# Graph network kernel: sorted message rows in bins padded to 512 rows, returned 1024 rows at a time

## What is computed

```python
def _L2_gnn_ref(x, bases, comps, alpha, edge_index, edge_type):
    row, col = edge_index[0], edge_index[1]          # src, dst
    deg = jax.ops.segment_sum(ones, row, num_segments=n)
    deg_inv = where(deg > 0, rsqrt(maximum(deg, 1.0)), 0.0)
    norm = deg_inv[row] * deg_inv[col]
    h_j = x[col]
    c_e = comps[edge_type]
    hj_b = c_e[:, :, None] * h_j[:, None, :]
    msg = jnp.einsum('ebd,bdf->ef', hj_b, bases)
    msg = msg * alpha[edge_type] * norm[:, None]
    return jax.ops.segment_sum(msg, row, num_segments=n)
```

## Time and profile before

| | us |
|---|---|
| three runs | 8993.05, 9007.82, 9013.69 |
| median | 9007.82 |
| the profiled execution, its own time | 8996.33 |
| its span in the trace | 8994.6 |

### The profile page before, as it was taken

The page is one execution under the profiler, slowest core; times in us unless marked ns, Lnnn a source line. Parts: engine busy times, 40 slices in busy tenths (PEclk is TensorE's granted clock), DMA queues, the critical chain, the costliest instruction groups (busy, mean ns, idle before and its releaser), DMA issues. The chain is left out here.

```text
span 8994.6 us, 165062 instructions
## 1 busy us (share of the span) xinstructions
PE 6838.9 (76%) x39312; PEld 5322.2 (59%) x39312; DVE 5025.3 (56%) x13644; ACT 1795.2 (20%) x5149; POOL 5985.1 (67%) x6303
## 2 busy tenths in 40 slices
PE   2766667676777777776777788886773899999997
PEld 2666566565555454454555577775662677777776
DVE  6445545455666666664222256654445567677666
ACT  1111111111222121222222222220002122222221
POOL 3777777776777777775777777772001777777774
PEclk7555555555767777777777799996665555555555
DMA  6344444443333333332222255553444333333332
GB/s 195 122 142 132 137 142 127 142 133 96 88 85 90 85 89 89 85 90 81 82 84 83 83 152 162 164 155 99 109 107 128 91 92 92 90 92 90 93 91 63
DMA packets 886407, 979.31 MB, mean 109 GB/s; under 512 B 139646, under 2 KB 711216, under 8 KB 886063
## 3 DMA queue, kind: packets, MB, share of 16 engines
q1 hardware_dynamic: 592437, 482.50, 18.3%
q0 software_dynamic: 200960, 418.41, 17.4%
q10 hardware_dynamic: 92794, 76.22, 2.8%
HBM read 649.26 MB, written 333.71 MB: 109 GB/s over the span
## 5 line engine op out<-in xcount | busy, mean ns | idle before, releaser
L2160 POOL DMA_INDIRECT soft_rows<-proj,soft_slot x1564 | 1501.1, 960 | 1269.5 <-ACT soft_slot L2181 823.6
L755 POOL DMA_INDIRECT L_rows<-H,L_slot x1568 | 1487.5, 949 | 613.3 <-issue 601.4
L1575 POOL DMA_INDIRECT sorted<-msg_out,msg_idx x1564 | 1497.9, 958 | 494.3 <-issue 451.4
L1029 POOL DMA_INDIRECT L_rows<-H,L_slot x1568 | 1484.6, 947 | 479.6 <-issue 437.7
L893 PE MATMUL L_sum<-L_onehot,L_rows 128*128 128x64 f32 x3136 | 705.9, 400 | 590.6 <-DMA L_rows<-H,L_slot 564.0
L1664 PEld LDWEIGHTS msg_ps_msg<-msg_hb,msg_lhs 128*128 128x128 f32 x6272 | 944.2, 238 | 194.1 <-issue 193.5
L893 PEld LDWEIGHTS L_sum<-L_onehot,L_rows 128*128 128x128 f32 x3136 | 648.6, 306 | 653.2 <-issue 497.5
L1619 DVE SCALAR_TENSOR_TENSOR msg_lhs<-msg_dst_sp,msg_node,msg_ps_c 128x512 f32<-128x512 f32 x784 | 550.6, 744 | 864.2 <-ACT msg_dst_sp L1588 805.0
L1664 PE MATMUL msg_ps_msg<-msg_hb,msg_lhs 128*128 128x128 f32 x6272 | 1031.7, 332 | 0.3 <-DVE msg_lhs L1619 0.3
L1673 PE MATMUL msg_ps_sum<-msg_back,msg_lo_hot 128*128 128x128 f32 x3936 | 699.0, 339 | 180.2 <-DVE sums_r L1639 154.1
L2289 PE MATMUL soft_ps_sum<-soft_onehot,soft_x 128*128 128x64 f32 x3136 | 752.2, 422 | 85.1 <-DVE sums_b L2406 82.4
(11 more groups left out here) (394 smaller groups left out, 11283.3 us busy)
## 6 DMA issues: line engine op xcount, KB each, us to landing
sorted<-L_zeros SPq DMA_DIRECT2D x394, 330.0 KB
msg_back<-sorted SPq DMA_DIRECT2D x492, 264.0 KB
L_rows<-H,L_slot POOLq DMA_INDIRECT x3136
msg_hb<-HB SPq DMA_DIRECT2D x392, 128.0 KB
soft_at_in<-in_edge_attr_dram SPq DMA_DIRECT2D x195, 256.0 KB
HB<-L_prod ACTq DMA_DIRECT2D x49, 512.0 KB, 3.0
sorted<-msg_out,msg_idx POOLq DMA_INDIRECT x1564
soft_rows<-proj,soft_slot POOLq DMA_INDIRECT x1564
```

The costliest lines, as they stand in the source:

```text
L755: pool.indirect_dma_start(rows[:, k, j, :], None, t["H0"], bass.IndirectOffsetOnAxis(ap=slot[:, k, j:j + 1], axis=0)).then_inc(gathered[k] ...
L1029: pool.indirect_dma_start(rows[:, k, j, :], None, t["H1"], bass.IndirectOffsetOnAxis(ap=slot[:, k, j:j + 1], axis=0)).then_inc(gathered[k] ...
L1575: pool.indirect_dma_start(t["sorted"], bass.IndirectOffsetOnAxis(ap=idx[:, s, j:j + 1], axis=0), out[:, s, j, :], None, **({} if w is None ...
L2160: pool.indirect_dma_start(rows[:, s % SC, j, :], None, t["proj"], bass.IndirectOffsetOnAxis(ap=slot[:, s, j:j + 1], axis=0)).then_inc(gath ...
```

## The change

- `UNIT` is 512 rows, and a block is one unit. A block is therefore one accumulation of four matmuls, one lookup in `unit_col`, and one addition.
- Because bins are padded to 512 rows, the table grows from 252,416 rows (492 blocks) to 301,568 rows (588 blocks). Each zeroing piece of phase 0 grows from 330 to 396 KB per group, and the pieces outside the loop go from three to one.
- `CUT` goes from 25/49 to 22/49 of the groups (group 200 to 176). The sets are 46 for the first part and 52 (312 blocks) for the second. The turns with blocks beside the groups begin at turn 46 of 98 instead of 52.
- `back` holds three pairs of blocks. One transfer brings 1024 rows (528 KB), issued at every second block, once the pair three before it has been multiplied.
- The lookup is taken out of `gain` into a step of its own (`find_columns`), ahead of `find_own`.
- The accumulator is set to zero after the groups of the first part instead of at the start of the phase.
- A few `nop`s on SP.

```diff
-UNIT = 2 * P
-BLOCK = 2 * UNIT
+UNIT = 4 * P
...
-        self.CUT = self.NGP // GB * 25 // 49
+        self.CUT = self.NGP // GB * 22 // 49
...
-        self.SETS = [-(-units // (2 * BQ)) for units in most]
-        self.BASE = [0, self.SETS[0] * BQ * BLOCK]
-        self.FIRST_UNIT = [0, self.SETS[0] * BQ * 2]
-        self.ROWS = sum(self.SETS) * BQ * BLOCK
+        self.SETS = [-(-units // BQ) for units in most]
+        self.BASE = [0, self.SETS[0] * BQ * UNIT]
+        self.FIRST_UNIT = [0, self.SETS[0] * BQ]
+        self.ROWS = sum(self.SETS) * BQ * UNIT
...
-        HI, NU = S.NT, max(S.SETS) * BQ * 2
+        HI, NU = S.NT, max(S.SETS) * BQ
...
-            link(v.tensor_scalar(units_i[:, :], units_i[:, :], 8, None, ALU.arith_shift_right))
+            link(v.tensor_scalar(units_i[:, :], units_i[:, :], 9, None, ALU.arith_shift_right))
...
-        back, lo_hot = sb("back", [P, R3, 4, WR]), sb("lo_hot", [P, R3, 4, P])
+        back, lo_hot = sb("back", [P, R3, 8, WR]), sb("lo_hot", [P, R3, 4, P])
...
             def return_rows(i, q):
-                b = i * BQ + q
-                sp.wait_ge(totalled, b + 1)
-                sp.nop(nofuse=True)
-                sp.dma_start(back[:, q % R3, :, :], tiles_of(t["sorted"], b * 4, 4)).then_inc(returned[q % R3], 16)
+                if q % 2 == 0:
+                    b = i * BQ + q
+                    sp.wait_ge(totalled, b + 2)
+                    sp.nop(nofuse=True)
+                    sp.dma_start(back[:, q // 2, :, :], tiles_of(t["sorted"], b * 4, 8)).then_inc(returned[q // 2], 16)
...
-            link(v.memset(acc, 0.0), False)
...
+            def clear_sums(turns, k):
+                if k < 2:
+                    v.memset(acc, 0.0).then_inc(prep, 1)
+                    v.wait_ge(prep, link.n + 1)
...
             def find_own(i, q):
                 b = i * BQ + q
-                v.wait_ge(returned[q % R3], (i * (BQ // R3) + q // R3) * 16 + 16)
-                v.wait_ge(totalled, b + 1)
+                v.wait_ge(returned[q // 2], i * 16 + 16)
+                v.wait_ge(totalled, b + 1 + BQ - R3)
...
+            def find_columns(i, q):
+                b = i * BQ + q
+                cols[q] = v.value_load(t["unit_col"][0:1, ds(b, 1)], min_val=0, max_val=(S.NT + 2) * P)
+
             def gain(i, q):
                 b = i * BQ + q
-                for u in range(2):
-                    at = v.value_load(t["unit_col"][0:1, ds(b * 2 + u, 1)], min_val=0, max_val=(S.NT + 2) * P)
-                    v.wait_ge(totalled, b + 1 + R3)
-                    v.wait_ge(gained, b * 2 + u + 2 * R2)
-                    v.tensor_tensor(acc[:, ds(at, P)], acc[:, ds(at, P)], ps_sum[q % R2][:, u * P:(u + 1) * P], ALU.add).then_inc(gained, 1)
-            with_blocks(v, S, t, [(0, make_lhs)], [(0, find_own), (2, gain)])
+                at = cols.pop(q)
+                v.wait_ge(totalled, b + 1 + BQ)
+                v.wait_ge(gained, b + R2)
+                v.tensor_tensor(acc[:, ds(at, P)], acc[:, ds(at, P)], ps_sum[q % R2][:, 0:P], ALU.add).then_inc(gained, 1)
+            with_blocks(v, S, t, [(0, make_lhs)], [(2, find_columns), (0, find_own), (2, gain)], after=clear_sums)
...
                 pe.wait_ge(hot_made, b + 1)
-                pe.wait_ge(gained, 2 * b + 2)
+                pe.wait_ge(gained, b + 1)
                 for k in range(4):
-                    mm = pe.matmul(ps_sum[q % R2][:, k // 2 * P:(k // 2 + 1) * P], lo_hot[:, q % R3, k, :], back[:, q % R3, k, 0:F],
-                                   start=(k % 2 == 0), stop=(k % 2 == 1))
+                    mm = pe.matmul(ps_sum[q % R2][:, 0:P], lo_hot[:, q % R3, k, :], back[:, q // 2, q % 2 * 4 + k, 0:F],
+                                   start=(k == 0), stop=(k == 3))
```

More of the change, by code:

```diff
@@ L1608, in _ @@
             v.sem_inc(lhs_made, R2)
-            v.sem_inc(gained, 2 * R2)
+            v.sem_inc(gained, R2)
+            cols = {}
+            def clear_sums(turns, k):
+                if k < 2:
+                    v.memset(acc, 0.0).then_inc(prep, 1)
+                    v.wait_ge(prep, link.n + 1)
             def make_lhs(i, r, w, s):
@@ L1623, in find_own @@
                 b = i * BQ + q
-                v.wait_ge(returned[q % R3], (i * (BQ // R3) + q // R3) * 16 + 16)
-                v.wait_ge(totalled, b + 1)
-                own, columns = bcast(back[:, q % R3, :, F], 2, P), bcast(ps_columns[:, 0:P], 1, 4)
+                v.wait_ge(returned[q // 2], i * 16 + 16)
+                v.wait_ge(totalled, b + 1 + BQ - R3)
+                own, columns = bcast(back[:, q // 2, q % 2 * 4:q % 2 * 4 + 4, F], 2, P), bcast(ps_columns[:, 0:P], 1, 4)
                 if t["widely"][0]:
@@ L1631, in find_own @@
                 make.then_inc(hot_made, 1)
+            def find_columns(i, q):
+                b = i * BQ + q
+                cols[q] = v.value_load(t["unit_col"][0:1, ds(b, 1)], min_val=0, max_val=(S.NT + 2) * P)
             def gain(i, q):
                 b = i * BQ + q
-                for u in range(2):
-                    at = v.value_load(t["unit_col"][0:1, ds(b * 2 + u, 1)], min_val=0, max_val=(S.NT + 2) * P)
-                    v.wait_ge(totalled, b + 1 + R3)
-                    v.wait_ge(gained, b * 2 + u + 2 * R2)
-                    v.tensor_tensor(acc[:, ds(at, P)], acc[:, ds(at, P)], ps_sum[q % R2][:, u * P:(u + 1) * P], ALU.add).then_inc(gained, 1)
-            with_blocks(v, S, t, [(0, make_lhs)], [(0, find_own), (2, gain)])
-            v.wait_ge(gained, 2 * NB + 2 * R2)
+                at = cols.pop(q)
[3 more added lines that the diff above has]
+            with_blocks(v, S, t, [(0, make_lhs)], [(2, find_columns), (0, find_own), (2, gain)], after=clear_sums)
+            v.wait_ge(gained, NB + R2)
         @block.tensor
@@ L1646, in _ @@
             pe.sem_inc(mixed, R4)
-            pe.sem_inc(totalled, R3)
+            pe.sem_inc(totalled, BQ)
             def spread_rows(i, r, w, s):
@@ L2608, in build_program @@
         t["bin_count"] = own("bin_count", [P, 2])
-        t["unit_col"] = own("unit_col", [1, S.FIRST_UNIT[1] + max(S.SETS) * BQ * 2], I32)
+        t["unit_col"] = own("unit_col", [1, S.FIRST_UNIT[1] + max(S.SETS) * BQ], I32)
         t["widely"] = [False]
```

## The result

| | before | changed |
|---|---|---|
| median, us | 9002.33 (4 runs) | 8786.65 (4 runs) |
| lowest to highest | 8993.05 to 9013.69 | 8784.78 to 8790.06 |
| ratio | | 0.976 (95%: 0.9743 to 0.9777) |
| the profiled execution, own time / span | 8996.33 / 8994.6 | 8790.06 / 8788.3 |
| first scatter to end of the last | 4168.4 to 6143.3 | 4157.4 to 6131.9 |

Measured again beside two other kernels, the changed one came to 8788.69 us (5 runs), ratio 0.9766 (0.9752 to 0.9779). The profiled executions differ by 206.3 us: 11.4 before the last scatter ends and 196.4 in the blocks alone, less 1.7 later (rounded).

What follows compares the result with a forecast made beforehand. Groups were taken as POOL-bound, the blocks alone mostly as bound by VectorE's sequencer. 8996.3 - 171 (blocks alone) - 10 (memset) = 8815 us profiled; with the median 11.5 above, 8827 us, 0.8 range 8775 to 8935.

Steps and rivals of the forecast that it cites:

- What bounds the old step: Blocks alone: of 2.465 us per step, VectorE's sequencer takes 2.07, the DMA 0.25, a rest 0.15.
- Lookup 0.72 us, sequencer ahead of the queue: VectorE, per block: a lookup costs 0.72 us, and the sequencer can do it while older operations run.
- a floor of 1.14: VectorE's sequencer in the new step: lookup 0.72, comparison 0.21, addition 0.21, together 1.14 us.
- Rival A: Blocks alone: the sequencer doesn't get ahead, the lookup is moved but not hidden; step 1.63 us, kernel 8914; chance 0.16.
- The DMA ring, 6T = 4.1 + T + 2.13, T = 1.25: Blocks alone, step T: pair landing 4.1 us, one step, then 2.13 until TensorE is done, over six steps: 1.25 us.
- The rest of 0.10 us: Blocks alone: added to the ring's 1.25 us because resources lie close, making the step 1.35 us.
- the old rest of 0.15: Blocks alone before the change: 0.15 us of the 2.465 us step, shared out among the other waits.
- Clock: TensorE in the blocks alone: full speed, 1.16 us per block, PEclk above 0.9 instead of 0.66.
- Rival C: Blocks alone: TensorE stays at 1.2 GHz, 2.08 us a block, kernel slower at 9054 us; chance 0.05.
- Rival B: Blocks alone: returns can't pass 154 GB/s, step 1.76 us, stretch 556 us, kernel 8955 us; chance 0.09.
- The memset: Accumulator zeroing, 10.83 us at the phase's start: 10 us less there, nothing at its new place.
- Zeroing a larger table, more blocks beside groups: Phase 0's 66 KB more per group, and 276 instead of 252 blocks under POOL: no cost forecast.

Runs made afterwards that it cites:

- the added wait: The changed kernel, with VectorE's sequencer made to wait behind each addition until that addition has ended: 8960.29 us.
- six singles: The changed kernel, with each block coming back by itself into a ring of six buffers instead of three pairs: 8757.06 us.
- an experiment: The changed kernel with six single-block buffers of returned rows instead of three pairs, DMA share alone 0.89: 8757.06 us.

## Why the prediction was right, point by point

- **Direction, size and range.** 8827 us (8775 to 8935) was predicted, 8786.65 measured: 216 us less (9002.33 − 8786.65) instead of the 181 that the prediction gave against the median shown then (9007.82). Between the profiled executions it was 206: 196 in the blocks alone for 171 predicted, and 11 before them for 10.
- **What bounds the old step.** Right: with more buffers and nothing else it fell to 2.163, close to the 2.07 read off the timeline.
- **Lookup 0.72 us, sequencer ahead of the queue.** Right here (undisturbed step 1.11 against a floor of 1.14; addition 0.60 after the comparison). It was incomplete as a rule: a wait that isn't met stops the sequencer, which the added wait and the moved lookups of the kernel before both showed. Rival A's mechanism is real, but had its place elsewhere than I put it. The queue of 8, strictly in order, that the Trainium skill gives VectorE (page "TensorE: Matmul & The Clock Gate", section "Architectural detail") says nothing of such stops; the measurements decide.
- **The DMA ring, 6T = 4.1 + T + 2.13, T = 1.25.** The mechanism was right: VectorE waits for rows more than for anything else, with a ring of three the step grew to 1.779, with six singles the wait vanished. That the value came so close to 1.270 is in part luck. In the changed kernel's blocks alone a round is 4.1 us from issue to the first comparison, 1.11 to the second (not T), and 2.4 from there to the next issue (not 2.13, SP's own 0.2 us were left out): 7.6 us for six steps. The two errors nearly cancel.
- **The rest of 0.10 us.** This is the term that was mis-sized: over the ring's 1.25 it measured 0.02. 311 steps of the difference are 25 us, nearly the whole distance between the predicted 429 us and the measured 403 alone. What the old rest of 0.15 was made of I didn't know, and had no reason to carry it over. The runs show one part: the loop's turn at each set of six, which makes that step 2.52 us for some 2.1 in the kernel before with a ring of six, or 0.07 to 0.08 per step. The new loop has it as well (0.065 per step with six singles), but as I read the ring's sum it isn't added to the round while the ring binds. The remainder stays open.
- **Clock.** Full speed was forecast, and PEclk was 0.99, with PE busy 343 of 390 us. Rival C is out. The busy share, by which the forecast argued, doesn't foretell the level: with the added wait PE was busy only 190 of 300 us and the granted clock 0.97, with the ring of three single blocks 193 of 300 and 0.99, while the kernel before had 219 of 300 and 0.67. By the Trainium skill (page "TensorE: Matmul & The Clock Gate", section "What's actually happening") the clock is lowered by default and activity releases it; the trace agrees, from 0.66 to 0.99 with the same matmuls packed closer.
- **Rate.** 212 GB/s at a share of 0.83, 230 at 0.89 in an experiment. Rival B, a cap at 154, is out. It could have been priced lower: the page of the profile before already shows 195 GB/s in its first slice, outside the stretches of the earlier trace rows. The bound worked out from the share, 248, was slightly low: 231 at a share of 0.90 point to some 257 (231 / 0.90, an estimate). The rate never became the bound. By the fit that the Trainium skill gives for a POOL-issued DMA (page "DMA: Bandwidth & Descriptors", section "Anatomy of one DMA") a pair would land in an estimated 3.2 us; this pair is issued by SP, and 4.16 passed until its first comparison.
- **The memset.** Predicted 10, measured 11.2 at the start and nothing at the border.
- **Zeroing a larger table, more blocks beside groups.** Nothing, as predicted. That the changed kernel would lose 17 us beside the groups with a ring of three was not foreseen.

## What to carry to other kernels

Add up what an engine's sequencer does per turn (register loads, address and threshold arithmetic, 0.2 us per operation) beside what the engine does; if the first is longer, fewer and larger operations can pay even where they bring padding, here 30% more blocks alone for half the lookups and additions per block. Count the loop's own turn too, here 0.39 us per set of six. The sequencer worked ahead as long as no unmet wait stood in its way, so put its long items just behind an operation, and not behind a wait for something just issued. Size a return ring by its depth in time (landing plus use, divided by the step), the issuing engine's own time included, and try many small buffers in place of few large ones: here six singles took 1.177 us a step, three pairs 1.270.

## What the runs showed of the hardware that was not expected

- A VectorE sequencer stopped by an unmet semaphore wait (on its own, ahead of a no-op) keeps the next register load from overlapping: 0.57 us per block, from 1.270 to 1.843. Ahead of an addition the stop was 0.54 us, ended 0.04 us after the addition waited for.
- The engine named as the last releaser need not be the bound: TensorE ended 213 of VectorE's waits in 300 us, and with half its matmuls the step was 1.174 for 1.177.
- The granted clock fell to 0.81 when half of the matmuls were taken away at the same step (PE busy 216 of 300 us), from 1.00 (284 of 300).
